# The last batch's x_pre summed by accumulating transfers, late tiles through two buffers and first in order, and the first x and weights on one queue

## What is computed

```python
h = einsum('bsi,boi->bso', x, weight[adapter_ids])            # 512x2048 @ 2048x2048, per batch
h_norm = h * rsqrt(mean(h * h, -1) + eps)
H_res, H_pre, H_post = sinkhorn(h_norm @ W_res.T + ..), softmax(h_norm @ W_pre.T + ..), softmax(.. W_post ..)
H_res = (1 - g) * I + g * H_res                               # 4x4 per token
x_pre = einsum('btnc,btn->btc', h_streams, H_pre)             # 4 streams -> 1
y = x_pre @ W_branch                                          # 512x512
out = x + einsum('btij,btjc->btic', H_res, h_streams) + y[:, :, None, :] * H_post[..., None]
```

## Time and profile before

| | |
|---|---|
| median of three runs | 1719.82 us |
| profiled execution | 1717.58 us |
| its span, first to last instruction | 1715.8 us |
| PE busy | 1686.2 us, 98% |
| DVE busy | 1425.7 us, 83% |
| ACT busy | 719.8 us, 42% |
| POOL busy | 101.5 us, 6% |
| mean granted TensorE clock | 0.995 |

### The profile page before, as it was taken

One profiled execution on the slowest core, in us unless ns is written; L12 is line 12 of the kernel. 1 busy time (PEld: TensorE's weight loads), 2 busy tenths in 40 slices (PEclk: granted clock), 3 DMA queues, 4 the chain that ended last, 5 costly groups with the idle time before them and its releaser, 6 DMA issues.

```text
span 1715.8 us, 24502 instructions
## 1 busy us (share of the span) xinstructions
PE 1686.2 (98%) x7740; PEld 1363.0 (79%) x7740; DVE 1425.7 (83%) x5973; ACT 719.8 (42%) x1167; POOL 101.5 (6%) x142
## 2 busy tenths in 40 slices
PE   8999999999999999999999999999999999999886
PEld 7888888888888878887888888888788887888773
DVE  4322499988998889988899979998899889998795
ACT  4433544244333343434433354424433454334563
POOL 0000000010000100000000000001000110001021
PEclk9999999999999999999999999999999999999999
DMA  6223423375233832358325562337522693238779
GB/s 238 87 92 125 152 87 111 99 216 189 99 109 113 253 140 98 103 151 264 99 90 128 186 212 98 111 102 218 187 96 87 168 317 101 89 97 217 175 136 247
DMA packets 68865, 252.41 MB, mean 147 GB/s; under 512 B 7936, under 2 KB 8064, under 8 KB 67840
## 3 DMA queue, kind: packets, MB, share of 16 engines
q1 hardware_dynamic: 48576, 177.97, 31.6%
q0 software_dynamic: 19584, 71.31, 17.5%
q10 hardware_dynamic: 576, 1.57, 0.3%
HBM read 203.63 MB, written 42.99 MB: 144 GB/s over the span
## 4 chain that ended last, share of the span: by engine, by line
PE 89%; issue 4%; DMA 3%; DVE 3%; POOL 1%; ACT 1%; SPq 0%; DVEq 0%; POOLq 0%; ACTq 0%
PE acc L1169 77%; PE y_ps L1247 3%; PE turn_ps L1205 3%; PE logit_ps L1213 2%; PE logit_ps L1216 2%; DVE piece L1027 2%; DMA x_raw<-xn 1%; DMA piece<-xn 1%; DMA out<-late_own 1%; DVE w_lo L778 1%; PE acc L1356 1%; PE y_ps L1237 1%; POOL out L427 1%; PE acc L1194 0%; PE turn_ps L1225 0%
## 5 line engine op out<-in xcount | busy, mean ns | idle before, releaser
L1169 PE MATMUL acc<-w_hi,x_hi 128*128 128x512 f32 x2040 | 807.7, 396 | 0.0
L1169 PE MATMUL acc<-w_hi,x_lo 128*128 128x512 f32 x2040 | 796.0, 390 | 0.0
L1169 PE MATMUL acc<-w_lo,x_hi 128*128 128x512 f32 x2040 | 794.4, 389 | 0.0
L473 ACT ACTIVATE w_hi<-w_raw 128x1024 fp32r<-128x1024 f32 x255 | 269.3, 1058 | 441.6 <-DMA w_raw<-wt 441.5
L1169 PEld LDWEIGHTS acc<-w_hi,x_lo 128*128 128x128 f32 x2040 | 382.9, 188 | 82.3
L1169 PEld LDWEIGHTS acc<-w_hi,x_hi 128*128 128x128 f32 x2040 | 383.2, 188 | 79.6
L1169 PEld LDWEIGHTS acc<-w_lo,x_hi 128*128 128x128 f32 x2040 | 383.6, 188 | 76.7
L778 DVE TENSOR_TENSOR w_lo<-w_raw,w_hi 128x1024 fp32r<-128x1024 f32 x256 | 311.7, 1218 | 133.8 <-ACT w_hi L473 122.4
L1027 DVE SCALAR_TENSOR_TENSOR piece<-cond,kern,piece 128x512 f32<-128x512 f32 x416 | 283.1, 746 | 5.0 <-DMA piece<-xn 5.0
L963 DVE RECIPROCAL vec<-vec 128x8 f32<-128x8 f32 x1536 | 240.4, 198 | 0.0
L961 DVE TENSOR_REDUCE vec<-work 128x8 f32<-128x32 f32 x1536 | 238.0, 194 | 0.2
(11 more groups left out here) (161 smaller groups left out, 835.7 us busy)
## 6 DMA issues: line engine op xcount, KB each, us to landing
w_raw<-wt SPq DMA_DIRECT2D x255, 512.0 KB, 3.5
out<-piece POOLq DMA_DIRECT2D x62, 512.0 KB, 5.4
x_raw<-xt SPq DMA_DIRECT2D x61, 512.0 KB, 5.4
piece<-xn POOLq DMA_DIRECT2D x56, 512.0 KB, 7.1
out<-late_own POOLq DMA_DIRECT2D x10, 512.0 KB, 9.0
grouped<-cond SPq DMA_DIRECT2D x16, 256.0 KB, 9.4
x_raw<-xn POOLq DMA_DIRECT2D x8, 512.0 KB, 12.0
out<-x_raw SPq DMA_DIRECT2D x7, 512.0 KB, 10.9
```

What stands on the lines that cost most here:

```text
L473: nc.scalar.activation(w_hi[:, unit % HI_SLOTS, :, :], w_raw[:, unit % LO_SLOTS, :, :], ACT.Copy).then_inc(w_hi_ready, 1)
L1169: mm = nc.tensor.matmul(acc[t][:], stationary, moving, start=(chunk == 0 and m == 0), stop=(chunk == CHUNKS - 1 and m == 2))
```

## The change

At the start the transfers of x move from ACT's queue to SP's: the two halves of the first piece before the adapter's number is read, the others behind the first weights, one piece of x and one of weights in turn. The warm-up has 32 transposes for 24, and unit 1 is ordered by product as unit 0 was. DVE makes the low part of unit 1's weights before that of its x.

In the ending the four weighed streams of a tile are no longer summed by PE: POOL adds streams 1, 2 and 3 onto stream 0 by three accumulating transfers of 256 KB from SBUF to SBUF (`sum_pre`), each waiting for the one before of its tile, and PE turns one tile (4 matmuls for 16). Late tiles use two buffers in turn (`cond_t`, `xpre_t`), x_pre has its own (`end_t`, over `xpre`). PE and ACT do late tiles 0 to 5 first; x_pre tiles follow between and behind the rest.

```diff
@@ -59,7 +59,8 @@
-WARM_UP = 24
+BY_PRODUCT = 2
+WARM_UP = 32
@@ -199,6 +201,8 @@
+        end_t = nc.alloc_sbuf_tensor_at("end_t", [P, 2, C], F32R, offset=xpre_place)
+        late_parts = (cond_t, xpre_t)
@@ -351,19 +356,22 @@
-                adapter = adapter_of(b)
...
+                    for k in range(UNIT_CHUNKS):
+                        sp.dma_start(x_raw[:, k, :], xt[0, :, k * TOKENS:(k + 1) * TOKENS]
+                                     ).then_inc((x_first_in, x_in[0])[k], 16)
+                    adapter = adapter_of(b)
...
-                        if u >= FIRST_X:
-                            load_x(b, u)
+                        load_x(b, u)
...
+                    adapter = adapter_of(b)
@@ -429,6 +437,18 @@
+            def sum_pre(t, j):
+                pool.wait_ge(pre_weighed, (t + 1) * STREAMS)
+                if j > 1:
+                    pool.wait_ge(pre_summed[t], (j - 1) * 16)
+                nc.gpsimd.dma_start(end_term[:, 0, t, :], end_term[:, j, t, :], accum_op=ALU.add
+                                    ).then_inc(pre_summed[t], 16)
+            def add_late_tile(k):
+                add_late(2 * k)
+                add_late(2 * k + 1)
@@ -448,21 +468,29 @@
-            for r in range(LATES * MIX_PAIRS):
-                add_late(r)
+            sum_pre(0, 1)
+            sum_pre(1, 1)
+            sum_pre(0, 2)
+            sum_pre(2, 1)
+            sum_pre(1, 2)
+            add_late_tile(0)
+            sum_pre(0, 3)
+            sum_pre(3, 1)
+            sum_pre(2, 2)
+            sum_pre(1, 3)
+            add_late_tile(1)
+            sum_pre(3, 2)
+            sum_pre(2, 3)
+            add_late_tile(2)
+            sum_pre(3, 3)
+            for k in range(3, LATE_TILES):
+                add_late_tile(k)
...
-            for k in range(UNIT_CHUNKS):
-                act.dma_start(x_raw[:, k, :], xt[0, :, k * TOKENS:(k + 1) * TOKENS]
-                              ).then_inc((x_first_in, x_in[0])[k], 16)
-            for u in range(1, FIRST_X):
-                act.dma_start(x_raw[:, 2 * u:2 * u + 2, :],
-                              xt[u, :, :].rearrange("p (k s) -> p k s", k=UNIT_CHUNKS)
-                              ).then_inc(x_in[u], 16)
@@ -525,13 +553,15 @@
-                    nc.scalar.activation(xpre_t[:, 0, :], y_ps[t % 2][:], ACT.Copy
+                    else:
+                        act.wait_ge(late_turned, TILES)
+                    nc.scalar.activation(end_t[:, 0, :], y_ps[t % 2][:], ACT.Copy
...
-                    nc.scalar.activation(xpre_t[:, 1, :], y_ps[t % 2][:], ACT.Copy
+                    nc.scalar.activation(end_t[:, 1, :], y_ps[t % 2][:], ACT.Copy
@@ -553,21 +583,23 @@
-                def late_high(k):
+                def late_halves(k):
+                    parts = late_parts[k % 2]
...
-                    if k == 0:
+                    if k < 2:
...
-                        act.wait_ge(late_y_ready, k)
-                    nc.scalar.activation(cond_t[:, 0, :], late_turn[k][:], ACT.Copy
+                        act.wait_ge(late_y_ready, k - 1)
+                    nc.scalar.activation(parts[:, 0, :], late_turn[k][:], ACT.Copy
...
-                def late_low(k):
...
-                    nc.scalar.activation(cond_t[:, 1, :], late_turn[k][:], ACT.Copy
+                    nc.scalar.activation(parts[:, 1, :], late_turn[k][:], ACT.Copy
...
+                def pre_halves(t):
+                    pre_high(t)
+                    pre_low(t)
@@ -613,34 +645,42 @@
-                late_high(0)
-                late_low(0)
+                late_halves(0)
...
+                late_halves(1)
...
+                late_halves(2)
+                weigh_streams(1)
+                late_halves(3)
+                weigh_streams(2)
...
-                for t in range(TILES):
-                    late_high(2 * t + 1)
-                    if t == 2:
-                        answer_log_step(asks, 1)
-                    pre_high(t)
-                    if t > 0:
-                        copy_y(t - 1)
-                    late_low(2 * t + 1)
-                    pre_low(t)
-                    if t + 1 < TILES:
-                        weigh_streams(t + 1)
-                        late_high(2 * t + 2)
-                        late_low(2 * t + 2)
-                        spread_late(2 * t)
-                        spread_late(2 * t + 1)
-                spread_late(LATE_TILES - 2)
-                spread_late(LATE_TILES - 1)
+                spread_late(0)
+                late_halves(4)
+                weigh_streams(3)
+                spread_late(1)
+                late_halves(5)
+                spread_late(2)
+                late_halves(6)
+                spread_late(3)
+                pre_halves(0)
+                late_halves(7)
+                spread_late(4)
+                answer_log_step(asks, 1)
+                copy_y(0)
+                pre_halves(1)
+                spread_late(5)
+                copy_y(1)
+                pre_halves(2)
+                spread_late(6)
+                copy_y(2)
+                pre_halves(3)
+                spread_late(7)
...
-                copy_y(TILES - 1)
+                copy_y(3)
@@ -1088,9 +1128,9 @@
-                        x_low(b, u)
...
+                        x_low(b, u)
@@ -1174,25 +1214,26 @@
-            def first_unit():
+            def unit_by_product(u):
...
-                        if m == 0 and k == 0:
+                        if m == 0 and k == 0 and u == 0:
...
-                        if m == 0 and k == 1:
-                            pe.wait_ge(x_hi_ready, 1)
-                            pe.wait_ge(w_hi_ready, 1)
+                        elif m == 0:
+                            pe.wait_ge(x_hi_ready, u + 1)
+                            pe.wait_ge(w_hi_ready, u + 1)
...
-                            pe.wait_ge(w_lo_ready, 1)
+                            pe.wait_ge(w_lo_ready, u + 1)
...
-                            pe.wait_ge(x_lo_ready, 1)
+                            pe.wait_ge(x_lo_ready, u + 1)
+                        chunk = UNIT_CHUNKS * u + k
...
-                            stationary = (x_lo if m == 2 else x_hi)[:, k, rows]
-                            moving = (w_lo if m == 1 else w_hi)[:, 0, k, :]
+                            stationary = (x_lo if m == 2 else x_hi)[:, chunk, rows]
+                            moving = (w_lo if m == 1 else w_hi)[:, u, k, :]
...
-                                                  start=(m == 0 and k == 0), stop=False)
+                                                  start=(m == 0 and chunk == 0), stop=False)
@@ -1268,27 +1309,25 @@
-                def turn_terms(t):
-                    pe.wait_ge(pre_weighed, (t + 1) * STREAMS)
+                def turn_last_pre(t):
+                    pe.wait_ge(pre_summed[t], (STREAMS - 1) * 16)
...
-                        for j in range(STREAMS):
-                            mm = nc.tensor.matmul(y_ps[t % 2][:, cols], end_term[:, j, t, cols],
-                                                  ident[:], start=(k == 0 and j == 0),
-                                                  stop=(k == C // P - 1 and j == STREAMS - 1),
-                                                  skip_group_check=True)
+                        mm = nc.tensor.matmul(y_ps[t % 2][:, cols], end_term[:, 0, t, cols],
+                                              ident[:], start=(k == 0), stop=(k == C // P - 1),
+                                              skip_group_check=True)
...
-                    nc.tensor.matmul(y_ps[t % 2][:], minus_ident[:], xpre_t[:, 0, :],
+                    nc.tensor.matmul(y_ps[t % 2][:], minus_ident[:], end_t[:, 0, :],
@@ -1338,12 +1377,12 @@
-                    multiply(cond_t, acc[k % TILES]).then_inc(late_y_ready, 1)
+                    multiply(late_parts[k % 2], acc[k % TILES]).then_inc(late_y_ready, 1)
...
-                    multiply(xpre_t, y_ps[t % 2]).then_inc(y_ready, 1)
+                    multiply(end_t, y_ps[t % 2]).then_inc(y_ready, 1)
@@ -1387,25 +1426,27 @@
+                turn_late(1)
...
-                turn_late(1)
-                turn_terms(0)
-                for t in range(TILES):
-                    late = 2 * t + 1
-                    take_late(late)
-                    if t != 2:
-                        take_pre(t)
-                    if late + 1 < LATE_TILES:
-                        turn_late(late + 1)
-                    branch_late(late)
-                    if t == 2:
-                        take_pre(t)
+                for k in range(1, 6):
+                    take_late(k)
+                    turn_late(k + 1)
+                    branch_late(k)
+                turn_last_pre(0)
+                take_late(6)
+                take_pre(0)
+                turn_late(7)
+                branch_late(6)
+                branch_last(0)
+                turn_last_pre(1)
+                take_late(7)
+                branch_late(7)
```

(10 more changed lines are left out.)

8 lines of the change are left out of this document (5 added, 3 removed).

## The result

The changed kernel took 1724.69 us (median of 11 runs, 1721.35 to 1726.59), the kernel before 1719.82 on the same chip. The ratio is 1.0028, with a 95% interval of 1.0018 to 1.0038: 4.9 us slower, where 1718.4 was forecast with a range up to 1724. The profiled execution took 1725.53 us, with a span of 1723.4.

A forecast was written before the change was run, and what follows sets the result against it. PE, busy 1686.2 of 1715.8 us, was taken as the bound, idle only at the two ends, with transfers bounding the close. Start 3.7 us gained, ending 2.3 lost: 1719.82 - 1.4 = 1718.4 us; 8-in-10 range 1713.5 to 1724.

The forecast's parts named there:

- The start: Up to unit 0's end: weights land sooner, first product at 8.2 us for 9.77, clock stays high; 3.7 us gained.
- rival 2: At the start: a gap over 1.6 us lowers the clock before the first product; gain 1.6 us, total 1720.5; chance 0.2.
- The ending: After the last large matmul: sums delay ACT's `log_step` answer, DVE stands 10.1 us, matrices come late; 2.3 us lost.
- with sums and landings free, ACT still comes to the `log_step` at 1651.3: In the ending: the new order by itself delays ACT to 1651.3; the ending then gains 1.5 us.
- the price of the sums: Accumulating transfers in the ending: 1.25 us per 256 KB sum, 15 us in all; ACT at the `log_step` at 1655.1.
- a fall of the clock once, at the close: PE's idle of 5.8 us before `spread_matrix` lowers its clock, taken as 2.0 us lost.
- The base sums hardly move: PE's base sums in the ending start at 1676.0 for 1675.6.
- 5.8 us of PE idle before `spread_matrix`: In the ending: fourteen base sums end at 1688.0, then PE idles 5.8 us for DVE's matrices, ready at 1693.8.
- Rival 3: Ending: double-price sums block ACT through five places; at 1.9 us each, `log_step` at 1660.9, total 1724.2; chance 0.15.
- accumulates into SBUF at 205 GB/s are no dearer than others: Argument from a window of the ending's transfers against sums at double price; 205 GB/s makes 1.28 us of 256 KB.
- Rival 1: Ending: sums cost 0.62 us or fall into idle engines; ending gains 1.5 us, total 1714.6; chance 0.2.
- Rival 4: Ending: ACT answers by 1647, DVE is not held up, the last accumulate decides; total 1710.9; chance 0.07.

The follow-up runs named there:

- the ending alone: The changed kernel with the start of the kernel before, so only the new ending; 1727.60 us, ratio 1.0056 to the kernel before.
- the answer early: The changed kernel with ACT's answer to the second `log_step` moved ahead of `spread_late(3)`; ratio 1.0015 to the kernel before.
- the two kernels whose `copy_logits` come first: Changed kernel with `grouped` issued after x_pre tile 0's sums, 1.0079; changed kernel with x_pre tile 0 and `log_step` answer ahead of `spread_late(3)`, 0.9991.
- the one where it comes last: The changed kernel without the twelve accumulating sums, x_pre being stream 0 alone; ratio 0.9978 to the kernel before.
- the start-only kernel: The kernel before with only the new start, its ending unchanged; 1715.51 us, ratio 0.9979 to the kernel before.
- the last kernel of section 5: New start and old ending, late tile 5's low half and x_pre tile 2's high half ahead of the `log_step`, 14 base sums before `spread_matrix`; 1711.23 us, 0.9951.

## Why the prediction was wrong

**The start: right in size, in part by luck.** Forecast 3.7 us gained; alone it gave 0.21% (0.12 to 0.31%), 3.6 us. The first product came at 7.39 for 8.2, and unit 2 started 4.2 us earlier relative to the kernel before (18.99 for 17.71 + 5.45). The wait from issue to landing fell to 2.7 us. The clock held, but not as forecast: PE was to idle from 6.6 to 8.2, safely short, and in the trace it did not idle at all, as the 32 transposes took 6.10 us and not 5.1. So rival 2, a fall of the clock in a longer gap, was not put to the test. The Trainium skill (DMA: Bandwidth & Descriptors, "Queues, rings and completion order") says that each engine goes round robin between the queue rows it has work for; the 5.8 us beside ACT's x and 2.7 without it, like the first sum's 10.2 us beside `grouped` for 3.3 without, agree with that. Which of the start's edits (queue, number of transposes, order by product, DVE's order) brings how much was not separated.

**The ending: the mechanism right, two terms mis-sized.** Forecast 2.3 us lost. The difference of the two ratios, 1.0028 and 0.9979, is 8.4 us, the ending alone 9.6, and the profiled pair has 8.0 from the last `copy_logits` to the end. The forecast's links, all set to the clock of the kernel before (0.36 us added to the changed kernel's rows):

| link | forecast | measured | late by |
|---|---|---|---|
| `spread_late(3)` ends | 1643.3 | 1648.0 | 4.7 |
| low half of late tile 7 ends | 1652.7 | 1658.9 | 6.2 |
| `log_step` on ACT | 1655.1 | 1661.0 | 5.9 |
| matrices ready | 1693.8 | 1699.9 | 6.1 |
| base sums start on PE | 1676.0 | 1685.1 | 9.1 |
| last add ends | 1712.9 | 1720.6 | 7.7 |

Two terms failed on the way of ACT to the `log_step`: the step "with sums and landings free, ACT still comes to the `log_step` at 1651.3", where 1654.4 was measured, and the price of the sums on top of it, 3.8 us forecast and 6.6 measured.
- *The order's own cost, counted with the sums away.* Without any sum ACT came at 1654.4, 3.1 us later than that. 2.8 of it are PE's slow turn and product behind its wait of 3.58 us. I priced a fall of the clock once, at the close, and not at the waits that my own schedule had in the middle. The granted clock was 0.82 over 1626 to 1645 of the changed kernel, where the kernel before had 1.00.
- *The sums' cost.* From 1654.4 to 1661.0 it is 6.6 us, for 3.8 forecast (1655.1 - 1651.3). The measured 1.52 us for 1.25 is 0.27 on each; on nine sums ahead of late add 2 that is 2.4 us, close to the 2.8 missing; this is an estimate, as no run changed the price of a sum. I had written that 0.25 on each would be worth 2.2.
- *The same 5.9 us along the changed kernel's own chain.* 4.7 of them are there when `spread_late(3)` ends, before PE is asked; the slow turn and product behind it (1.91 and 3.60 us for 1.05 and 2.88) add 1.6. So in this kernel the late landing is the larger part and the clock behind this wait the smaller; how the 5.9 divide exactly is not shown.
- *The close.* From the matrices to the last add's end the forecast had 19.1 us with 2.0 for the clock, the trace 20.8: `spread_matrix` and the two sums behind it take 1.97 and 3.73 us for 1.00 and 1.94. The last store then took 3.1 us for 5.1. So 6.1 + 1.7 - 2.0 = 5.8, which is, but for rounding, 8.0 less the forecast's 2.3.

**"The base sums hardly move": wrong, and it hid behind the other strand.** They moved 9.1 us. Of these 5.9 are the `log_step`'s, behind which x_pre tile 1 stands on ACT, and 2.6 are that tile's product at the lower clock (5.49 us for 2.88), which had no term in the sum. The forecast's 5.8 us of PE idle before `spread_matrix` were 2.57. That is why the answer early brought 2.2 us, though it took 16 us off DVE's wait.

**The rivals.** Rival 3 had the right mechanism, place and time of the `log_step` (1660.9, total 1724.2; measured 1661.0 and 1724.69), but said it decides only from 1.8 us a sum on, and its numbers are for 1.9. They were reached at 1.52, as the clock fell in the middle as well; that they agree so closely is luck. The reason against it, "accumulates into SBUF at 205 GB/s are no dearer than others", misreads its row: of the 12 transfers issued in that stretch 5 are late adds into `out`, not into SBUF, several ran at once, and no sum was ever seen by itself. Rival 1 (cheap sums) fell with the 172 GB/s, and its 1.5 us of gain was not seen even without any sum (0.9978 against 0.9979 for the old ending), though the intervals are too wide to exclude it. The Trainium skill's 435 GB/s (DMA: Bandwidth & Descriptors, "Where 436 GB/s comes from") would make an estimated 0.6 us of a sum; the trace has 1.52. Rival 4 fell with DVE's 16.44 us.

**Chances.** Rival 3 had 0.15 and the sum was called sensitive, but the range ended at 1724, inside that rival. Two errors of one sign, neither large, were enough to pass it.

**What stays open.** Of the 4.7 us by which `spread_late(3)` was late, an estimated 2.4 are the price of nine sums; how the rest divides between the mix with `grouped` and POOL's order was not measured, since moving `grouped` changed both. Why the large products end up to 4.5 us apart in profiled executions of the same code is known in part. PE does wait inside them, for DVE's `cond_t` and ACT's `acc`: 1.8 us in the kernel before, so its idle time is not all at the two ends, as the prediction has it; 2.1 us in the two kernels whose `copy_logits` come first (1600.47 and 1601.65), 5.1 us in the one where it comes last (1604.95). A lead from the start may be lost in such waits. What makes them differ from one execution to the next stays open.

## What to carry to other kernels

An instruction that waits for a transfer's place sits in an in-order engine like a gate: before putting anything on which a second engine depends behind it, ask whether it can stand ahead. Before moving work from a busy engine to transfers, ask whether they have room when the work is due; here two strands were late, and freeing one showed the other. When a schedule contains waits of an engine whose clock can fall in them, put a price on the fall at each of them, and measure a new kind of transfer by itself before nine of them stand in a chain.

## What the runs showed of the hardware

- An accumulating transfer of 256 KB from SBUF to SBUF took 1.52 us of all 16 engines and landed 3.3 us after issue with nothing beside it. With `grouped` and late adds beside it the median was 8.3 us and the longest 12.3.
- 12 such sums raised the share of the DMA engines over 1605 to 1665 from 0.73 to 1.02 (0.29 of 60 us is 17.4 us; 12 x 1.52 is 18.2), and PE's busy time there fell from 53.6 to 40.9 us:

```profile
1605.00:1665.00 60.00, 53.64 (x313) 46.13 (x313) 56.21 (x456) 37.89 (x71) 10.14 (x12) 0.97 0.73 139
```
```profile
1605.00:1665.00 60.00, 40.86 (x194) 32.94 (x193) 40.51 (x321) 33.83 (x64) 19.45 (x22) 0.89 1.02 191
```

The first row is the kernel before, the second the changed one. Some 10 us of PE's fall are the matmuls removed; the granted clock, third column from the end, shows the other loss: 0.97 and 0.89.
- PE's granted clock fell to its lower level, 1.2 GHz, after waits of 2.57, 3.58 and 6.87 us; a product then took up to 5.49 us for 2.88. After the wait of 2.31 us in the kernel before it fell too; after the one of 2.12 us at the same place of the start-only kernel it did not, which is one reason that its ending is 1.8 us shorter. The length of one wait does not settle it: in the last kernel of section 5 a wait of 2.62 us before `spread_matrix` left the clock at 1.00, and of two waits of 2.30 us in the changed kernel the one that ended at 1625.06 left the next turn at 1.05 us, the one at 1631.56 made it 1.91.
